# First rows in two loads with two interleaved chains of statistics, gated weights in three parts, and last additions on VectorE, in a one-core feed-forward and random-feature kernel

## The reference, cut to what matters

```python
xn = layernorm(x)                                    # over 256
# random features: weights (256 x 256) and rows
feats   = exp(xis) / 16 * exp(xn @ (xis * proj).T - 0.5 * |xn|^2 * xis^2)
weights = the same of input_weights
s = feats @ weights.T
# feed-forward on ternary weights with a scale per output
h = silu((xn @ w1.T) * w1_s) * ((xn @ w2.T) * w2_s)  # 256 -> 1024
h = gelu((h @ h1.T) * h1_s)                          # 1024 -> 1024
h = gelu((h @ h2.T) * h2_s)                          # 1024 -> 1024
g = silu((h @ w3.T) * w3_s)                          # 1024 -> 256
out = x + s * g
```

## Time and profile before

| what | value |
|---|---|
| median of 3 runs | 1306.65 us (1306.61 to 1307.64) |
| profiled execution | 1305.47 us |
| its span, first to last instruction | 1303.6 us |
| TensorE matmuls busy | 1292.8 us (99%), 6100 |
| VectorE busy | 939.1 us (72%), 1191 |
| ScalarE busy | 752.7 us (58%), 1006 |
| GpSimd (POOL) busy | 764.9 us (59%), 791 |
| granted TensorE clock, mean | 0.999 of 2.4 GHz |

### The profile page before, as it was taken

One profiled execution on the slowest core, in us unless ns is written; L12 is line 12 of the kernel. 1 busy time (PEld: TensorE's weight loads), 2 busy tenths in 40 slices (PEclk: granted clock), 3 DMA queues, 4 the chain that ended last, 5 costly groups with the idle time before them and its releaser, 6 DMA issues.

```text
span 1303.6 us, 16277 instructions
## 1 busy us (share of the span) xinstructions
PE 1292.8 (99%) x6100; PEld 1071.2 (82%) x6100; DVE 939.1 (72%) x1191; ACT 752.7 (58%) x1006; POOL 764.9 (59%) x791
## 2 busy tenths in 40 slices
PE   8999999999999999999999999999999999999998
PEld 7788888888888887888878888788897888878887
DVE  7887768787588875878668686677857777456675
ACT  4566644766456664465645656456555565455664
POOL 6961015899569994699846898368973791040000
PEclk9999999999999999999999999999999999999999
DMA  9697735545265552654517454275542754313441
GB/s 353 242 359 239 236 99 153 193 149 175 80 156 173 177 167 69 170 172 156 165 65 190 161 167 145 81 186 163 166 132 81 197 171 136 107 65 129 132 159 52
DMA packets 96836, 207.50 MB, mean 159 GB/s; under 512 B 13936, under 2 KB 16240, under 8 KB 95728
## 3 DMA queue, kind: packets, MB, share of 16 engines
q1 hardware_dynamic: 80032, 157.11, 36.4%
q0 software_dynamic: 16720, 49.30, 13.5%
HBM read 174.87 MB, written 37.78 MB: 163 GB/s over the span
## 4 chain that ended last, share of the span: by engine, by line
PE 96%; DVE 3%; ACT 0%; DMA 0%; issue 0%
PE ps L219 73%; PE ps L222 23%; DVE split L202 1%; DVE quad L202 0%; DVE quad L212 0%; PE ps L307 0%; DMA xin<-in_x 0%; ACT split L198 0%; DVE sm L212 0%; ACT quad L198 0%; DVE sm L202 0%; DVE xin L208 0%; DVE st L262 0%; DVE st L263 0%; DVE xT L202 0%
## 5 line engine op out<-in xcount | busy, mean ns | idle before, releaser
L219 PE MATMUL ps<-split,ring 128*128 128x512 f32 x2800 | 763.7, 390 | 0.3 <-DVE split L202 0.3
L219 PEld LDWEIGHTS ps<-split,ring 128*128 128x128 f32 x2800 | 525.6, 188 | 109.9 <-DVE split L202 0.7
L202 DVE TENSOR_TENSOR split<-quad,split 128x1024 fp32r<-128x1024 f32 x258 | 340.5, 1330 | 186.8 <-ACT split L198 185.7
L222 PE MATMUL ps<-split,ring 128*128 128x512 f32 x784 | 305.0, 389 | 0.0
L198 ACT ACTIVATE split<-quad 128x1024 fp32r<-128x1024 f32 x258 | 266.5, 1052 | 43.2 <-PE ps L222 43.1
L219 PE MATMUL ps<-xT,w 128*128 128x512 f32 x766 | 219.9, 395 | 0.7 <-ACT xT L198 0.6
L597 POOL TENSOR_TENSOR cube<-cube,seen 128x256 f32<-128x256 f32 x176 | 207.1, 1177 | 14.3
L862 POOL TENSOR_TENSOR ry<-ry,s 128x256 f32<-128x256 f32 x56 | 40.6, 757 | 242.8 <-ACT ry L198 242.8
L198 ACT ACTIVATE quad<-ps 128x512 f32<-128x512 f32 x193 | 114.4, 596 | 117.6 <-PE ps L222 117.5
L198 ACT ACTIVATE quad<-quad,cols 128x512 f32<-128x512 f32 (+1 forms) x194 | 137.6, 717 | 66.9 <-DVE quad L202 64.7
L219 PEld LDWEIGHTS ps<-xT,w 128*128 128x128 f32 x766 | 143.2, 188 | 35.3 <-issue 3.3
(11 more groups left out here) (99 smaller groups left out, 1235.3 us busy)
## 6 DMA issues: line engine op xcount, KB each, us to landing
ring<-hs SPq DMA_DIRECT2D x428, 256.0 KB, 3.5
xin<-in_x SPq DMA_DIRECT2D x17, 512.0 KB, 3.2
s_h<-s SPq DMA_DIRECT2D x16, 512.0 KB, 6.1
seen<-in_h POOLq DMA_DIRECT2D x64, 128.0 KB, 2.8
ry<-in_x SPq DMA_DIRECT2D x15, 512.0 KB, 4.8
out<-ry SPq DMA_DIRECT2D x15, 512.0 KB, 2.6
hs<-in_h SPq DMA_DIRECT2D x6, 1024.0 KB, 7.8
z_h<-xin POOLq DMA_DIRECT2D x48, 128.0 KB, 4.3
```

What stands on the lines that cost most here:

```text
L202: return dve.mark(lambda e: e.tensor_tensor(dst, a, b, op))
L219: pe.run(lambda e: e.matmul(dst, stat, mov, start=start, stop=stop, skip_group_check=loose))
L222: return pe.mark(lambda e: e.matmul(dst, stat, mov, start=start, stop=stop, skip_group_check=loose))
```

## The change

- The first half tile comes in two loads of 256 KB (blocks 0 and 1, blocks 2 and 3), each with a semaphore of its own.
- Its statistics are two chains on two blocks each (`first_stats`), written alternately into VectorE's list; the first is ahead by four entries.
- SP sends the projection and the input weights after a wait for the second of these loads; `load_x(1)` follows them.
- The rows are turned ahead of the projection and the input weights on TensorE; `WARM` is 20.
- Of half tile 0, ScalarE makes the high part of feature half 0, VectorE (`vcopy`) that of feature half 1. In every half tile both high parts are now written ahead of the low parts, and the first gated step waits for both.
- w1 and w2 come in three parts each (`W12`): columns of steps 0 and 1, 2 and 3, 4 to 7. POOL waits for the second parts before it goes on.
- `turn_rows(1, ...)` moves from ahead of step 5 to ahead of step 6, its copies to ahead of step 7.
- At the end VectorE adds all four blocks, in another order of steps.

```diff
-WARM = 16
+
+W12 = [(0, 2), (2, 4), (4, 8)]
+WARM = 20
...
+        d_x0 = [port(f"d_x0{i}") for i in range(2)]
...
+        def first_stats():
+
+            def chain(part):
+                cols2 = slice(2 * part, 2 * part + 2)
+                var, y, u, q = (sm[:, i, cols2] for i in range(4))
+                b0, b1 = 2 * part, 2 * part + 1
+                dve.wait(d_x0[part].token)
+                dve.run(lambda e: e.bn_stats(st[:, b0, :], xin[0][:, b0, :]))
+                a = dve.mark(lambda e: e.bn_stats(st[:, b1, :], xin[0][:, b1, :]))
+                yield
+                dve.wait(a)
+                dve.run(lambda e: e.bn_aggr(mv[:, b0, :], st[:, b0, :]))
+                a = dve.mark(lambda e: e.bn_aggr(mv[:, b1, :], st[:, b1, :]))
+                yield
...
+                for _ in range(3):
+                    a = vst(u, y, -0.5, y, ALU.mult, ALU.mult, a)
+                    yield
+                    a = vv(u, u, var, ALU.mult, a)
+                    yield
+                    a = vst(y, u, 1.5, y, ALU.add, ALU.mult, a)
+                    yield
+                for b in (b0, b1):
+                    xn_done[0, b] = vs(xin[0][:, b, :], xin[0][:, b, :], mv[:, b, 0:1], sm[:, 1, b:b + 1], ALU.subtract, ALU.mult, a)
+                    yield
...
+            chains = [chain(0), chain(1)]
+            for _ in range(4):
+                next(chains[0])
+            while chains:
+                for one in reversed(chains[:]):
+                    if next(one, "end") == "end":
+                        chains.remove(one)
...
+            hi = [None] * KD
             for kd in range(KD):
-                hi = xT_hi[h] = cast(xT[j][:, kd, 0, :], ps[:, banks[kd], :], turned[kd], *xT_free.get(h - 2, []))
-                xT_lo[h] = vv(xT[j][:, kd, 1, :], ps[:, banks[kd], :], xT[j][:, kd, 0, :].bitcast(F32), ALU.subtract, hi)
+                make = vcopy if h == 0 and kd else cast
+                hi[kd] = make(xT[j][:, kd, 0, :], ps[:, banks[kd], :], turned[kd], *xT_free.get(h - 2, []))
+            xT_hi[h] = hi
+            for kd in range(KD):
+                xT_lo[h] = vv(xT[j][:, kd, 1, :], ps[:, banks[kd], :], xT[j][:, kd, 0, :].bitcast(F32), ALU.subtract, hi[kd])
...
-        load_x(0)
+        for part in range(2):
+            d_x0[part].send(sp, xin[0][:, 2 * part:2 * part + 2, :], x_h[0][:, 2 * part:2 * part + 2, :])
         d_cols.send(sp, cols[:, :], cols_in)
+        sp.wait(d_x0[1].token)
         d_pj.send(sp, pj, proj.rearrange("(a p) d -> p a d", p=P))
         d_wi.send(sp, wi, win.rearrange("(a p) d -> p a d", p=P))
-        sp.wait(d_x[0].token)
-        for half in range(2):
+        for part, (begin, end) in enumerate(W12):
             for n, (name, w) in enumerate((("w1", w1), ("w2", w2))):
-                d_w12[2 * n + half].send(pool, w[:, :, half * T:(half + 1) * T], w_kpm[name][:, :, half * T:(half + 1) * T])
+                d_w12[n][part].send(pool, w[:, :, P * begin:P * end], w_kpm[name][:, :, P * begin:P * end])
         load_x(1)
...
-            pool.wait(d_w12[0].token, d_w12[2].token)
+            pool.wait(d_w12[0][1].token, d_w12[1][1].token)
...
         scale_proj()
+        first_stats()
+        copy_first = turn_rows(0, (0, 1))
         turn_proj()
-        for task in stats_tasks([0]):
-            task()
-        copy_first = turn_rows(0, (0, 1))
         copy_proj()
...
-                side[5] += [lambda: copies1.append(turn_rows(1, (0, 1))), lambda: norms_in(0)]
-                side[6].append(lambda: copies1[0]())
+                side[6] += [lambda: copies1.append(turn_rows(1, (0, 1))), lambda: norms_in(0)]
+                side[7].append(lambda: copies1[0]())
...
-            if b < 2:
-                pool.wait(made_y[b], d_x[0].token)
-                a = pool.mark(lambda e: e.tensor_tensor(x0, x0, yt[:, b, :], ALU.add))
-            else:
-                a = vv(x0, x0, yt[:, b, :], ALU.add, made_y[b], d_x[0].token)
+            a = vv(x0, x0, yt[:, b, :], ALU.add, made_y[b], d_x[0].token)
...
-        for step, b in ((scaled, 0), (scaled, 1), (gated_y, 0), (added, 0), (scaled, 2), (gated_y, 1), (added, 1), (scaled, 3),
-                        (gated_y, 2), (added, 2), (gated_y, 3), (added, 3)):
+        for step, b in ((scaled, 0), (scaled, 1), (gated_y, 0), (added, 0), (gated_y, 1), (scaled, 2), (added, 1), (scaled, 3),
+                        (gated_y, 2), (gated_y, 3), (added, 3), (added, 2)):
```

More of the change, by code:

```diff
@@ L296, in stats_tasks @@
             return out
+        def first_stats():
[11 more added lines that the diff above has]
+                yield
+                v = vs(var, mv[:, cols2, 1], 1e-5, None, ALU.add, None, a)
+                yield
+                a = vs(y.bitcast(I32), var.bitcast(I32), 1, None, ALU.logical_shift_right, None, v)
+                yield
+                a = vs(y.bitcast(I32), y.bitcast(I32), -1.0, RSQRT_SEED, ALU.mult, ALU.add, a)
+                yield
[3 more added lines that the diff above has]
+                    a = vv(u, u, var, ALU.mult, a)
+                    yield
+                    a = vst(y, u, 1.5, y, ALU.add, ALU.mult, a)
+                    yield
+                for b in (b0, b1):
+                    xn_done[0, b] = vs(xin[0][:, b, :], xin[0][:, b, :], mv[:, b, 0:1], sm[:, 1, b:b + 1], ALU.subtract, ALU.mult, a)
+                    yield
+                a = vv(q, mv[:, cols2, 1], y, ALU.mult, a)
+                yield
+                last = vst(q, q, -0.5 * D, y, ALU.mult, ALU.mult, a)
+                norm_done[0] = lambda: last
+            chains = [chain(0), chain(1)]
[5 more added lines that the diff above has]
+                        chains.remove(one)
         def turn_rows(h, banks):
@@ L358, in w12_ready @@
         def w12_ready(m):
-            return [d_w12[2 * n + m // Q].token for n in range(2)]
+            part = [begin <= m < end for begin, end in W12].index(True)
+            return [d_w12[n][part].token for n in range(2)]
         def gated_step(h, m, pair, dst, *tokens):
             j = h % 2
-            pe.wait(xT_hi[h], *w12_ready(m), *free[pair[0]])
+            pe.wait(*xT_hi[h], *w12_ready(m), *free[pair[0]])
             parts = [[[(w[:, k, m * P:(m + 1) * P], xT[j][:, k, g, :]) for k in range(KD)] for g in range(2)] for w in (w1, w2)]
```

6 lines of the change are left out of this document (3 added, 3 removed).

## The result

The change is slower, by about as much as a measurement can tell: 1308.81 us (median of 19 runs, 1307.46 to 1309.50) where the kernel before gave 1306.27 beside it (19 runs). The ratio is 1.0019, 95% interval 1.0013 to 1.0025, so +1.7 to +3.3 us. The forecast was -1.7, with a range of 1303.9 to 1306.7.

What follows compares the result with a forecast made beforehand. TensorE's stream was taken to set the time. Start -1.0, stop near 23 us -0.8 and end +0.1 summed to -1.7 us, taking the median from 1306.65 to 1304.95, range 1303.9 to 1306.7.

Steps and rivals of the forecast that it cites:

- First rows: At the start, two loads and two interleaved statistics chains end the fourth block's normalisation at 8.85 against 9.80, 0.95 earlier.
- rival 2: VectorE's start: the two chains do not overlap, a pair costs 0.40, not 0.20; whole +0.35, 1307.0; chance 0.05.
- rival 3: First rows land early, second half at 3.8; the start follows by 0.5, whole -2.2, 1304.45; chance 0.15.
- The input weights "just in time": Start: projection lands at 7.6 and input weights at 9.8, when TensorE wants the latter, though SP sends them later.
- Rival 1: Input weights landing at 10.5 to 11.45 hold low matmuls to 12.0 to 12.95; whole -1.1 to -0.1, middle 1306.0; chance 0.22.
- High and low parts by two engines: Start: about 0.65 per copy, high parts run 9.27 to 9.95, lows end near 11.25; VectorE's added copy costs nothing.
- Sum of the start: First gated matmul that reads a low part starts at 11.35 against 12.40, -1.0.
- The stop, -0.8: TensorE's 0.81 us wait near 23 us, ahead of turning the second half tile, is covered by turning one gated step later.
- Rival 4: The stop near 23 us stays: VectorE keeps its old times or falls behind, 0.8 not won; 1305.75; chance 0.08.
- Cost 0: Second half tile's rows land at 11.5 to 12.5 where VectorE would take them at 11.3, at no cost.
- Gated weights, 0: w1 and w2 in three parts: the smaller first part keeps POOL from binding the first gated matmul; otherwise 0.
- The end, +0.1: Behind the last matmul, VectorE's last addition ends at 1300.10 against 1300.03, the last output 0.33 later; bounds -0.2 and +0.5.

Runs made afterwards that it cites:

- early_proj_old_tail: The change with the old end, SP sending projection and input weights at once, before its wait for x's second half: 1305.88 us against 1306.36, ratio 0.9999.
- start_only: The change with the old end and the second turning where it was: 1308.98 us against 1306.39 for the kernel before, ratio 1.0023.
- after_old_tail: The change with the end of the kernel before: 1308.15 us against 1306.39 for the kernel before, ratio 1.0020.
- after_pins_off: The change with the old end, first tile's t4 subtractions behind t1's split, next tile's rows requested near 52 us: 1305.90 us against 1306.09, ratio 0.9998.
- rows_highs: Kernel before with second turning a step later, t4 subtractions later, next rows earlier, and high parts by two engines: 1304.69 us against 1306.09, ratio 0.9990.
- move_only: Kernel before with only the turning of half tile 1 moved from ahead of step 5 to step 6: 1306.34 us against 1306.39, ratio 0.9998.
- pool_late: Kernel before with 1.4 us of scratch clears on POOL ahead of its first sums: 1308.82 us against 1306.36, ratio 1.0018.
- w12_only: Kernel before with only w1 and w2 in three parts each: 1306.64 us against 1306.36, ratio 1.0001.
- good_start: The change with old end, projection and input weights sent at once, w1 and w2 in halves, head start two entries: 1307.24 us against 1306.03, ratio 1.0009.
- tail_only: Kernel before with only the change's end, VectorE adding all four blocks in the new order: 1306.60 us against 1306.39, ratio 1.0003.
- t4_rows_move: Kernel before with second turning a step later, first tile's t4 subtractions later, next tile's rows requested near 52 us: 1305.03 us against 1306.03, ratio 0.9992.
- x_split_only: Kernel before with only its first rows in two 256 KB loads instead of one of 512 KB: 1306.45 us against 1306.09, ratio 1.0003.
- pool_early_move: Kernel before with second turning a step later and POOL not waiting for the second half tile's statistics: 1311.79 us against 1306.36, ratio 1.0041.

## Why the prediction was wrong, step by step

- **First rows, -0.95 to the last normalisation: measured -0.2.** Of its terms the pace was right: the second chain goes from its first small operation at 6.00 to its normalisations at 8.87 in 2.87 us, where 2.4 + 0.4 was put in; rival 2 did not happen. What failed is "its chain starts three steps ahead" as harmless: of the head start's four entries, each waiting for the one before, two (4.46 and 4.86) take 0.48 us ahead of the second chain's statistics, which start at 4.94 instead of 4.3, though their rows had landed by 4.13. The first half's landing at 3.39 was as needed. The formula cited for rival 3 from the Trainium skill ("DMA: Bandwidth & Descriptors", Anatomy of one DMA) is given there for DMAs that GpSimd issues. These loads are SP's, and took 2.6 and 2.9 us to landing where it gives 2.6.
- **The input weights "just in time": the step that turned the start.** The text put their landing at 9.8 and the projection's at 7.6, from spacings in a trace in which x is one load. They landed at 11.35 and 9.83. The first gated matmul stands behind the input weights' transposes and starts 0.41 behind their landing, at 11.76 where 10.3 was forecast; so it does, 0.4 behind the landing, in the four variants that keep this order of TensorE's list and the three parts (early_proj_old_tail, start_only, after_old_tail, after_pins_off). The projection's lateness moved ScalarE's high part too, as the text said it would once the cover was gone, but that ended at 11.21 and bound nothing. Rival 1 is thus right for the start, landing and mark (12.77 within its 12.0 to 12.95); its total of at most 1306.55 fails with the rest of the sum.
- **High and low parts by two engines: right in kind.** The high parts were to take 0.68 us together instead of 1.09. VectorE's copy took 0.69 (0.65 put in), and in rows_highs the first gated matmul gains 0.2 by it. That the copy "costs nothing" was 0.1 off: the low parts end that much later there.
- **Sum of the start: -1.0 forecast, +0.4 measured** (12.77 against 12.40).
- **The stop, -0.8: removed, and not won.** move_only shows both. Rival 4 has the gain not won, but by a stop that stays. The forecast checked only what stood within five us of the stop, and found "none" between 24 us and the last layer because it read waits over 0.5. The wait of 0.28 for the split at 80.46 was the sign that VectorE had no slack there: most of what TensorE gains earlier becomes a longer wait there.
- **The second half tile's rows late, "Cost 0", and POOL's loads with "10 us of cover": a term put at nothing.** The forecast let these rows land at 11.5 to 12.5; they landed at 13.4. VectorE took the rows 1.3 us later (13.39 against 12.06, where the load had been in since 11.5), and POOL's sums began 1.2 later. The text followed POOL's loads up to the first sum and stopped. What it had to follow is POOL's last sum near 78 us, which runs beside VectorE's split, and the ring pieces that TensorE meets there. pool_late prices it: 1.4 us on POOL cost 2.5 by the medians, and 1.5 in its traced execution.
- **Gated weights, 0:** right by w12_only, with x in one load; good_start suggests that with two loads their size counts. **The end, +0.1:** not contradicted; tail_only has +0.2 within -0.7 to +1.6. In the trace the last addition is 0.04 later behind the last matmul.
- **The chances.** "Slower by over 0.2% has no case here but a loss I don't see, 0.03." The loss was visible in kind. Two of the three signs in its last sentence came: TensorE's last wait at the start is for the input weights, and a wait for a ring load turns up later. The small operations, 0.08 apart, are the third and did not.

In sum, by medians against the kernel before: the changed start costs 1.8 us with the couplings near 80 us in place (after_old_tail against move_only), 0.8 without them (after_pins_off against t4_rows_move). So about 1.0 of it passes through POOL's lateness and the couplings, and the 0.8 of the stop is swallowed there as well. What the change's 2.5 has beyond that, 0.7, is its end or the error. These are differences of medians with errors near 1 us each, so the split is rough.

TensorE's clock is a rival for the loss, and not its cause here: the seven of the change's 19 executions with a mean clock of 0.999 have a median of 1308.55, 2.3 above before. But nine have 0.997, which none of the 130 executions of before timed beside the variants has, and these are not slower for it (median 1308.84). Why they are not isn't shown.

## What to carry to other kernels

A gain on the bounding engine counts only up to the next place where another engine or a load is just in time; look for its small waits (0.2 to 0.3 us) and price the edit past each of them. If an edit delays an engine off the path, follow that engine to where its run ends, not to where it starts. When executions of one kernel spread, look at the clock of each before guessing at loads. And when a load is split or sent later to free an early one, list every load behind it with who takes it first on each engine, in that engine's order.

## What the runs showed of the hardware

- Two loads of 256 KB (2 KB of each partition) in place of one of 512 KB (4 KB of each) left the last byte of x between 4.1 and 4.5 us (before 4.2) and the loads behind it about 2 us later. In x_split_only the DMA engines moved 153 and 210 GB/s in the two us from 3.5, against 224 and 283.
- The split of 128x1024 on VectorE takes 1.21 to 1.23 us (30 of them past 1180 us, where POOL is idle) and up to 2.72 beside POOL's sums (9 from 30 to 84 us, most of them beside sums, median 1.72), in the trace of before.
- In the stretch from 62 to 84 us of the change the DMA engines are full (share 1.01, 377 GB/s); a ring load of 256 KB lands 7.6 us after its issue there (median of 12), 3.5 over the whole run:

```profile
62.00:84.00 22.00, 20.57 (x89) 16.15 (x88) 18.43 (x21) 13.24 (x18) 18.96 (x16) 1.00 1.01 377
```

```profile
ring<-hs SPq DMA_DIRECT2D x12, 256.0 KB, 7.6
```

- Small VectorE operations that do not depend on each other start 0.08 us apart even where each waits for a semaphore, against 0.20 for one that waits for the one before it. The Trainium skill ("VectorE: DVE Perf Modes", The DRAIN you can't avoid) has the next operation wait for the empty pipe, and adds that one that is not held starts earlier. The rows at 6.00 and 6.08 show the second case: the later operation starts 0.18 us before the earlier one, 0.26 long, has ended.
- TensorE's clock fell to its lower level, 1.2 GHz, behind idle stretches of 1.28 and 0.44 us at the start of after_pins_off's traced execution (0.50 granted from 14 to 16 us) and behind 3.2 us near 28 us in pool_early_move (0.52 from 30 to 34). It stayed at the upper one behind 1.27 and 0.24 us in after_old_tail. All 15 executions of variants that took over 1310 us have a mean granted clock of 0.995 to 0.998.
